# A three-layer max-aggregation graph network: edge arrays moved to POOL's queue, the lane table to PSUM, 49 node tiles, a shorter carry

## The chip, the cores and the metric

The kernel runs on one core of one Trainium2 chip. The metric is device time in microseconds (us). The core has five engines with queues of their own: PE (TensorE, matmuls), DVE (VectorE), ACT (ScalarE), POOL (GpSimd) and SP (SyncE, which only issues DMAs here), and 16 DMA engines that all queues share. Engines meet through semaphores. SBUF and PSUM are the on-chip memories, both with 128 partitions.

## What is computed

There are 6250 nodes with 128 features and 200000 edges `(src, dst)` sorted by `dst`. Cut to what matters:

```python
def conv(x, src, dst, Wl, bl, Wr):
    agg = segment_max(x[src], dst, num_segments=6250)   # max over a node's incoming edges
    agg = where(isfinite(agg), agg, 0.0)                # nodes without edges
    return agg @ Wl + bl + x @ Wr

h = maximum(layernorm(x), 0.0)
h = leaky_relu(conv(h, src, dst, Wl1, bl1, Wr1), 0.01)  # 128 -> 256
h = leaky_relu(conv(h, src, dst, Wl2, bl2, Wr2), 0.01)  # 256 -> 256
h = leaky_relu(conv(h, src, dst, Wl3, bl3, Wr3), 0.01)  # 256 -> 128
return x + h
```

## The kernel before, in words

**Tiling.** The edge list is cut into 512 runs of 391 edges: four chains (`CHAINS`) of 128 partitions. One column of work is one edge from each of 128 runs, so a layer has 4 x 391 = 1564 columns. A column is fetched by one indirect DMA on POOL's queue (L343): 128 indices from `stage` choose 128 rows of the feature table in HBM, and they land in `ring`, which holds 56 columns in 7 blocks of 8. A step is one turn of the ring; a layer has 28 steps, the last with 52 columns. Over three layers that is 4692 gathers.

**The scan.** For each group of four columns DVE adds a restart row (0 or the lowest float, from `restart_ps` in PSUM) to the previous group, L617, writing PSUM, and takes the maximum with the new group, L638. SP writes each finished group to a log in HBM (L1014, L1018). DVE also copies the indices of later blocks into `stage` (L606).

**The picks.** In the first 25 steps of layer 0, DVE also builds, once a step, the matrices by which PE finds each node's run: `pick_from` (L586) compares the lane table `lane` (0 to 255, in SBUF) with `pick_bounds` (SBUF) and writes into `own`; `pick_not_below` (L593) does the same with the upper bounds; `pick_below` (L601) subtracts one from the other, in bf16. Each goes over 128 x 1024 elements.

**A layer's end.** When the log is complete, POOL gathers four `patch` tiles (L360). Beside it runs the carry from run to run: PE turns the last group (L845), DVE scans it (L703, `carry_scan`), DVE adds the row `join_row[:, 0]` to the scan shifted by one (L709, `incoming`), and PE turns it back (L851). DVE takes the maximum with `patch` (L713), SP stores it (L1025). Then POOL gathers the last log row of each node, one DMA for each tile of 128 nodes (L370), 50 tiles. Tiles go in pairs: PE turns (L864), DVE masks and guards (L721, L731), PE multiplies by `Wl` (L876), DVE adds the node's own part and takes the leaky ReLU (L738, L749, in the last layer L753 and L762), SP stores (L1031). POOL's next layer waits for all these stores.

**The start.** SP issues the five loads of `x` (L984, 640 KB each), with `dst` after the first (L986) and `src` after the last (L987), then eight loads of one word per run (L992, `prev_last` and `next_first`), nine loads of weights, two small stores, and the five stores of the normalised features (L1004), each when its ten tiles are done. DVE computes the statistics (L411, L414), ACT normalises 8 tiles of ten (L907) and DVE the other two (L428, L431). DVE then takes the differences that tell whether `dst` is sorted (L443, L445, L448), PE sums them over partitions (L786), and all engines that may have to sort read the answer. DVE lays out `src` (L511), fills `stage` (L513) and prepares bounds, restart rows and join rows (L519 to L567) while POOL may begin gathering. POOL's first gather waits for the five stores and for `stage`. The rows of `x` are padded to 6400, 50 tiles; `out` has as many rows.

POOL waits at the head of each block of eight gathers, which is this piece:

```python
pool.wait_ge(block_scanned, ...)
if not first:
    pool.wait_ge(logged[b], ...)
pool.sem_inc(gathers_open, 1)
```

## Time and profile before

| | us |
|---|---|
| median of 3 runs | 6219.27 (6217.3 to 6219.34) |
| the profiled execution | 6222.6 |
| its span, first to last instruction | 6220.9 |
| busy, POOL / DVE / PE / ACT | 4632.6 / 2902.1 / 706.5 / 232.1 |
| share of the 16 DMA engines, gathers' queue / SP's and ACT's | 31.0% / 23.2% |
| indirect DMAs issued by POOL: gathers L343 / patch L360 / ends L370 | 4692 / 12 / 150 |

The median comes from executions without a profile, the rows further down from the one profiled execution. "Busy" counts an instruction from its start to its end; for a DMA on POOL's queue this is the time in which POOL writes it out, not the time in which the bytes move. A row of the timeline gives the start, the duration, engine, line, operation, output and input, and in brackets how long the engine stood idle before it and what ended that. "issue" means that the profile shows nothing that the engine waited for.

### The profile page before, as it was taken

Reading aid. Unit: us, or ns where it says so; the run is one execution under the profiler, and the core shown is the slowest. Engines: PE = TensorE matmul, PEld = TensorE weight load, DVE = VectorE, ACT = ScalarE, POOL = GpSimd, SP = SyncE. Lnnn points to the kernel's source line nnn. Section 1 sums busy time; section 2 is a strip of 40 time slices with the busy share of each in tenths; the row PEclk is TensorE's granted clock in tenths of the full one; section 3 lists DMA queues with packets and bytes.
Section 4 is the critical chain, followed back from the end, with each engine's and each line's share of the span. In section 5 each row is a group of like instructions: output and inputs, shape, how many; then the busy total and the mean of one; then the engine's idle time right before and its main releaser. Section 6 shows DMA issues by size and latency. Waiting matters only on the chain. (4 is left out here: it accounts for less than half of the span.)

```text
span 6220.9 us, 24572 instructions
## 1 busy us (share of the span) xinstructions
PE 706.5 (11%) x2258; PEld 407.3 (7%) x2258; DVE 2902.1 (47%) x3636; ACT 232.1 (4%) x675; POOL 4632.6 (74%) x4861
## 2 busy tenths in 40 slices
PE   0110011111000680000000000047000000000003
PEld 0000000000000340000000000035000000000002
DVE  5333333333333555555555555565555555555556
ACT  1000000000000110000000000012000000000001
POOL 5777777777777677777777777767777777777776
PEclk8555555555555655555555555565555555555556
DMA  4333333333333576666666666667666666666665
GB/s 131 104 106 106 104 103 105 106 105 104 106 104 103 153 240 210 210 209 212 209 211 209 210 209 209 211 195 252 209 211 209 209 210 209 209 210 211 209 211 166
DMA packets 436613, 1089.93 MB, mean 175 GB/s; under 512 B 101509, under 2 KB 155018, under 8 KB 436586
## 3 DMA queue, kind: packets, MB, share of 16 engines
q0 software_dynamic: 207104, 530.50, 31.0%
q1 hardware_dynamic: 206266, 539.48, 23.2%
q10 hardware_dynamic: 23216, 19.67, 1.0%
q14 instruction: 20, 0.16, 0.0%
q8 instruction: 7, 0.11, 0.0%
HBM read 555.78 MB, written 533.46 MB: 175 GB/s over the span
## 5 line engine op out<-in xcount | busy, mean ns | idle before, releaser
L343 POOL DMA_INDIRECT ring<-features,stage x4692 | 4475.1, 954 | 1491.1 <-issue 1384.2
L638 DVE TENSOR_TENSOR ring<-banks,ring 128x1024 f32<-128x1024 f32 (+1 forms) x1173 | 1226.2, 1045 | 3093.4 <-DMA ring<-features,stage 3076.0
L617 DVE TENSOR_TENSOR banks<-ring,banks 128x1024 f32<-128x1024 f32 (+1 forms) x1173 | 1232.4, 1051 | 37.6
L845 PE MATMUL banks<-ident,ring 128*128 128x128 f32 x20 | 5.0, 428 | 3755.5 <-DVEq L650 3755.5
L827 PE MATMUL banks<-dst_low,own 128*128 128x394 bf16 x200 | 99.2, 496 | 1492.7 <-DVE own L601 1492.7
L845 PEld LDWEIGHTS banks<-ident,ring 128*128 128x128 f32 x20 | 3.9, 222 | 3756.9 <-DVEq L650 3533.0
L811 PE MATMUL banks<-wr,h_turned 128*128 128x256 f32 (+1 forms) x500 | 207.3, 557 | 97.7 <-ACT h_turned L932 97.7
L975 ACT ACTIVATE agg<-zeros 128x512 f32<-128x512 f32 x75 | 47.3, 630 | 3962.2 <-PE banks L876 3962.2
L370 POOL DMA_INDIRECT ring<-running_max_log,end_row x150 | 145.2, 968 | 63.4 <-issue 44.8
L606 DVE COPY stage<-edges 128x8 int32 (+1 forms) x588 | 137.5, 234 | 84.9 <-DVE banks L617 25.8
L813 PE MATMUL banks<-b,ones 1*128 1x256 f32 (+1 forms) x300 | 143.7, 575 | 0.0
L811 PEld LDWEIGHTS banks<-wr,h_turned 128*128 128x128 f32 x500 | 122.7, 302 | 160.8 <-ACT h_turned L932 151.8
L827 PEld LDWEIGHTS banks<-dst_low,own 128*128 x200 | 27.6, 138 | 1536.1 <-issue 1534.4
L876 PE MATMUL banks<-wl,agg 128*128 128x256 f32 (+1 forms) x500 | 113.4, 370 | 2.0 <-DVE agg L731 1.9
L828 PE MATMUL banks<-dst_high,own 128*128 128x394 bf16 x200 | 97.9, 489 | 0.0
L803 PE MATMUL banks<-ident,h_in 128*128 128x128 f32 x250 | 85.4, 425 | 27.6 <-DMA h_in<-features 27.6
L948 ACT ACTIVATE signs<-banks,node 128x391 bf16<-128x391 f32 x50 | 29.4, 588 | 1571.4 <-PE banks L828 1571.3
L876 PEld LDWEIGHTS banks<-wl,agg 128*128 128x128 f32 x500 | 87.1, 213 | 12.0 <-DVE agg L731 5.0
L813 PEld LDWEIGHTS banks<-b,ones 1*128 1x128 f32 x300 | 67.4, 278 | 65.1 <-issue 65.1
L864 PE MATMUL banks<-ident,ring 128*128 128x128 f32 x250 | 60.4, 322 | 75.5 <-DMA ring<-running_max_log,end_row 73.3
L721 DVE TENSOR_SCALAR finite<-banks 128x512 int32<-128x512 int32 (+1 forms) x75 | 44.9, 598 | 47.1 <-PE banks L864 46.5
L941 ACT ACTIVATE own<-banks 128x256 f32 (+2 forms) x150 | 52.2, 348 | 367.4 <-PE banks L813 367.4
(104 smaller groups left out, 563.7 us busy)
## 6 DMA issues: line engine op xcount, KB each, us to landing
running_max_log<-ring SPq DMA_DIRECT2D x782, 512.0 KB, 3.3
running_max_log<-ring SPq DMA_DIRECT2D x391, 256.0 KB, 2.2
ring<-features,stage POOLq DMA_INDIRECT x4692, 2.8
features<-h_out SPq DMA_DIRECT2D x50, 256.0 KB, 2.3
h_in<-features ACTq DMA_DIRECT2D x100, 128.0 KB
ring<-x SPq DMA_DIRECT2D x5, 640.0 KB, 8.8
features<-ring SPq DMA_DIRECT2D x5, 640.0 KB, 7.2
h_in<-features ACTq DMA_DIRECT2D x50, 64.0 KB
```

Of the source, the lines that this page charges most:

```text
L343: pool.indirect_dma_start(ring[:, c * w:(c + 1) * w], None, tables[l], bass.IndirectOffsetOnAxis(ap=stage[:, b, u:u + 1].bitcast(U32), axi ...
L370: pool.indirect_dma_start(ring[:, t * w:(t + 1) * w], None, logs[w], bass.IndirectOffsetOnAxis(ap=end_row[:, t:t + 1].bitcast(U32), axis=0 ...
L606: dve.tensor_copy(stage[:, b, :], src_t[:, bass.ds((i + ahead) * RING_COLS + b * BLOCK_COLS, BLOCK_COLS)]).then_inc(block_scanned, 1)
L617: dve.tensor_tensor(sum_ps[:, 0:CHAINS * w].rearrange("p (h f) -> p h f", h=CHAINS), group(g - 1).rearrange("p (h f) -> p h f", h=CHAINS), ...
L638: dve.tensor_tensor(group(g), sum_ps[:, 0:CHAINS * w], group(g), ALU.max).then_inc(turn, 1)
L803: turn = pe.transpose(turn_ps[0][:, c * P:(c + 1) * P], h_in[p][:, c * P:(c + 1) * P], ident[:, :])
L811: pe.matmul(mm_ps[p][:, 0:n], h_turned[p][:, c, :], wr_sb[l][:, c, :], start=(c == 0), stop=False)
L813: pe.matmul(mm_ps[p][:, 0:n], ones[0:1, :], b_sb[l][:, :], start=False, stop=True).then_inc(own_mm, 1)
L827: pe.matmul(sel_ps[p][:, 0:RUN + 3], chosen, dst_low[:, h, :], start=(h == 0), stop=False)
L828: mm = pe.matmul(sel_ps[p][:, 0:RUN + 3], chosen, dst_high[:, h, :], start=False, stop=(h == CHAINS - 1))
L864: turn = pe.transpose(turn_ps[b][:, t * w + c * P:t * w + (c + 1) * P], ring[:, k * w + c * P:k * w + (c + 1) * P], ident[:, :])
L876: mm = pe.matmul(mm_ps[b][:, t * n:(t + 1) * n], agg[b][:, t * w + c * P:t * w + (c + 1) * P], wl_sb[l][:, c, :], start=(c == 0), stop=(c ...
```

## The change

- `x` is alone at the head of SP's queue, followed by the weights. `dst`, the neighbour words and `src` are issued by POOL. The eight neighbour loads become four: two of 127 partitions with four words each, two of three words.
- POOL takes the differences of neighbouring `dst` (int32 subtract, 128 x 1560 and 128 x 4). DVE takes their minimum and compares it with 0.
- ACT normalises 7 tiles of ten. The other three are POOL's now: three `tensor_scalar` and one maximum over 384 columns for each of the five shares. A first `Sqrt` of ACT stands before the wait for constants.
- `lane_ps`, a copy of the lane table, lies in PSUM bank 5 beside `restart_ps`; L586 and L593 read it in place of `lane`.
- `END_TILES` is 49: 49 gathers of ends in each layer, the last pair has one tile, and `own`, `h_in`, the intermediate tables and `out` follow.
- The carry: `joins` goes into `dst_high` (an offset of `NO_NODE` where a run doesn't join), so the row `join_row[:, 0]`, L709 and half of L562 to L567 go. `carry_scan` is one column longer, and PE turns it back directly.
- POOL opens each layer with one list of waits and then the gathers, without `sem_inc`; the first step of each layer is outside the loop; the waits for `h_stored` and `logged` are in reversed order; the `sem_inc` before L370 goes.

```diff
-ACT_TILES = 8
+ACT_TILES = 7
+    END_TILES = -(-nodes // P)
+    PAIR_TILES = [min(2, END_TILES - 2 * q) for q in range(PAIRS)]
...
+        lane_ps = banks[:, 5, BANK - 2 * P:BANK]
...
+            pool.dma_start(dst_runs, dst.rearrange("(h p) j -> p h j", p=P)).then_inc(order_loaded, DMA)
+            pool.wait_ge(const_done, 2)
+            with nc.allow_non_contiguous_dma(reason="one word of each run of edges"):
+                for dest, there in run_neighbours(dst):
+                    pool.dma_start(dest, there).then_inc(order_loaded, DMA)
+            pool.dma_start(src_runs.rearrange("p (h j) -> p h j", h=CHAINS),
+                           src.rearrange("(h p) j -> p h j", p=P)).then_inc(src_loaded, DMA)
+
+            pool.wait_ge(order_loaded, (LOADS - 1) * DMA)
+            pool.tensor_tensor(rises_runs[:, :, 1:RUN], dst_runs[:, :, 1:RUN], dst_runs[:, :, 0:RUN - 1],
+                               ALU.subtract).then_inc(order_checked, 1)
+            pool.tensor_tensor(rises_runs[:, :, 0], dst_runs[:, :, 0], prev_last[:, :],
+                               ALU.subtract).then_inc(order_checked, 1)
+
+            for s in range(TAIL_STEPS):
+                share = slice(s * TAIL_TILES + ACT_TILES, (s + 1) * TAIL_TILES)
+                pool.wait_ge(norm_ready, 2 * (s + 1))
+                for k in range(share.start, share.stop):
+                    pool.tensor_scalar(h0_all[:, k, :], x_all[:, k, :], rstd[:, k:k + 1], shift[:, k:k + 1],
+                                       ALU.mult, ALU.add).then_inc(h0_scaled, 1)
+                pool.wait_ge(h0_scaled, (TAIL_TILES - ACT_TILES) * (s + 1))
+                pool.tensor_scalar(h0_all[:, share, :], h0_all[:, share, :], 0.0, None,
+                                   ALU.max).then_inc(h0_rest_done, 1)
...
+                        for b in reversed(range(STORES)):
+                            pool.wait_ge(h_stored[b], PER_OUT * l)
+                        pool.wait_ge(block_scanned, SIGNED * l + 1)
+                        pool.wait_ge(logged[0], LOGGED[0] * l)
...
-                pool.sem_inc(ends_open, 1)
-                for t in range(TILES):
+                for t in range(END_TILES):
...
-                    dve.tensor_tensor(pick_slot(i), lane[:, :].unsqueeze(1).to_broadcast(across),
+                    dve.tensor_tensor(pick_slot(i), lane_ps.unsqueeze(1).to_broadcast(across),
...
                 for c in range(kc):
-                    dve.tensor_tensor_scan(carry_scan[:, c, :], join_row[:, 1, :],
+                    dve.tensor_tensor_scan(carry_scan[:, c, 1:RUNS + 1], pass_row[:, :],
                                            carry_ps[:, c * RUNS:(c + 1) * RUNS], 0.0,
-                                           ALU.add, ALU.max).then_inc(join_step, 1)
-                for c in range(kc):
-                    before = sum(s[0] for s in shapes[:l]) // P
-                    dve.wait_ge(join_step, before + c + 1)
-                    dve.tensor_tensor(incoming[:, c, 1:RUNS], carry_scan[:, c, 0:RUNS - 1],
-                                      join_row[:, 0, 1:RUNS], ALU.add).then_inc(incoming_ready, 1)
+                                           ALU.add, ALU.max).then_inc(carried_on, 1)
```

## Rows read from the trace of the kernel before

**Rows 1.** The page, groups by line: count, busy and mean ns, idle before by releaser
```profile
L343 POOL DMA_INDIRECT ring<-features,stage x4692 | 4475.1, 954 | 1491.1 <-issue 1384.2
```
**Rows 2.** Groups of POOL from 60 to 1805 us, then from 2130 to 4080 us
```profile
L343 POOL DMA_INDIRECT ring<-features,stage x1369 | 1329.5, 971 | 417.2 <-issue 376.1 <-DVE stage L606 41.1
...
L343 POOL DMA_INDIRECT ring<-features,stage x1560 | 1474.8, 945 | 475.2 <-issue 475.2
```
**Rows 3.** Timeline in step 24 of layer 0: start, us, engine, line, operation
```profile
1781.34 1.22 DVE L586 TENSOR_TENSOR own<-lane,pick_bounds 128x1024 f32 x1
1781.62 1.75 POOL L343 DMA_INDIRECT ring<-features,stage  x1 [0.30 <-issue]
...
1802.89 0.68 DVE L601 TENSOR_TENSOR own<-own,not_below 128x1024 bf16 x1
1803.15 1.24 POOL L343 DMA_INDIRECT ring<-features,stage  x1 [0.30 <-issue]
```
**Rows 4.** Timeline in layer 2: a gather beside the scan's maximum
```profile
6126.94 1.22 DVE L638 TENSOR_TENSOR ring<-banks,ring 128x1024 f32<-128x1024 f32 x1 [4.92 <-DMA ring<-features,stage]
6127.75 0.95 POOL L343 DMA_INDIRECT ring<-features,stage  x1 [0.30 <-issue]
```
**Rows 5.** Timeline in step 1 of layer 0: the one pick without a longer gather
```profile
139.33 1.26 DVE L586 TENSOR_TENSOR own<-lane,pick_bounds 128x1024 f32 x1
139.34 0.94 POOL L343 DMA_INDIRECT ring<-features,stage  x1 [0.31 <-issue]
```
**Rows 6.** Timeline of SP's queue at the start
```profile
13.39 4.54 SPq L992 DMA_DIRECT2D next_first<-dst  x1
...
25.51 8.21 SPq L1004 DMA_DIRECT2D features<-ring  x5
```
**Rows 7.** Stretches of the start: last three columns PEclk, DMA share, GB/s
```profile
2.00:18.00 16.00, 0.00 (x0) 0.00 (x0) 12.79 (x89) 6.24 (x15) 0.00 (x0) 1.00 1.09 303
18.00:22.00 4.00, 0.00 (x0) 0.00 (x0) 3.86 (x26) 3.47 (x11) 0.00 (x0) 1.00 0.17 11
22.00:26.00 4.00, 0.00 (x0) 0.00 (x0) 3.86 (x26) 3.47 (x11) 0.00 (x0) 1.00 0.82 235
26.00:38.00 12.00, 0.59 (x2) 0.50 (x2) 8.83 (x19) 5.44 (x15) 0.00 (x0) 1.00 0.98 280
```
**Rows 8.** Timeline of the start: ACT's last tiles, the order check, stage, the first gather
```profile
25.18 6.26 ACT L907 ACTIVATE ring<-ring,shift,rstd 128x128 f32<-128x128 f32 x16
...
27.32 1.78 DVE L443 TENSOR_TENSOR edges<-own 128x1560 f32<-128x1560 int32 x1
...
35.69 0.19 DVE L513 COPY stage<-edges 128x48 int32<-128x48 int32 x1
...
40.13 1.36 POOL L343 DMA_INDIRECT ring<-features,stage  x1 [38.65 <-DMA features<-ring]
```
**Rows 9.** Timeline: DVE's preparation beside the fourth gather
```profile
44.22 2.91 DVE L551 TENSOR_TENSOR edges<-own 128x1560 f32<-128x1560 int32 x1
44.41 4.53 POOL L343 DMA_INDIRECT ring<-features,stage  x1 [0.30 <-issue]
```
**Rows 10.** Timeline: POOL's widest elementwise instruction of before
```profile
0.98 0.34 POOL L261 IOTA lane_i<- 128x256 int32 x1 [0.40 <-POOLq L1067]
```
**Rows 11.** Timeline of layer 0's end: last two tiles on PE, last projection
```profile
2114.96 0.30 PE L864 MATMUL banks<-ident,ring 128*128 128x128 f32 x1 [0.90 <-DMA ring<-running_max_log,end_row]
...
2116.47 0.33 PE L864 MATMUL banks<-ident,ring 128*128 128x128 f32 x1 [1.21 <-DMA ring<-running_max_log,end_row]
...
2118.27 2.07 PE L876 MATMUL banks<-wl,agg 128*128 128x256 f32 x4 [0.59 <-DVE agg L731]
```
**Rows 12.** Groups with shapes apart: an end operation of DVE over two tiles and over half the width
```profile
L738 DVE TENSOR_TENSOR z_sum<-banks,own 128x512 f32<-128x512 f32 x50 | 34.0, 680 | 6.2 <-PE banks L876 6.1
...
L738 DVE TENSOR_TENSOR z_sum<-banks,own 128x256 f32<-128x256 f32 x25 | 10.2, 407 | 0.4 <-PE banks L876 0.3
```
**Rows 13.** Timeline of layer 2's end: the patch's maximum
```profile
6143.84 1.22 DVE L713 TENSOR_TENSOR patch<-patch,banks 128x1024 f32<-128x1024 f32 x1 [4.63 <-DMA patch<-running_max_log,patch_row]
```

More of the change, by code:

```diff
@@ L33, with gnn_program @@
 TILE_MASK = 0x7FFFFF80
-def gnn_program(nc, x, src, dst, weights, out):
+def gnn_program(nc, x, src, dst, weights, out, nodes):
     NODES, F_IN = x.shape
@@ L347, in gather @@
                             ).then_inc(landed[b], DMA)
-                if l == 0:
-                    gather(0, True, False)
-                with pool.Fori(1 if l == 0 else 0, STEPS - 1) as i:
+                gather(0, True, False)
+                with pool.Fori(1, STEPS - 1) as i:
                     gather(i, False, False)
                 gather(STEPS - 1, False, True)
-                for b in range(BLOCKS):
+                for b in reversed(range(BLOCKS)):
                     pool.wait_ge(logged[b], LOGGED[b] * (l + 1))
@@ L961, in keep_pair @@
                             count_run(j, p)
-                    for p in range(2):
-                        keep_turned(j, p, more)
+                    for p in range(PAIR_TILES[j] if isinstance(j, int) else 2):
+                        keep_turned(j, p, p < loads)
                         keep_own(j, p)
@@ L984, in _ @@
                 sp.dma_start(x_all[:, t, :], x_rows[:, t, :]).then_inc(x_loaded[s], DMA)
-                if s == 0:
-                    sp.dma_start(dst_runs, dst.rearrange("(h p) j -> p h j", p=P)).then_inc(edges_loaded, DMA)
-            sp.dma_start(src_runs.rearrange("p (h j) -> p h j", h=CHAINS),
-                         src.rearrange("(h p) j -> p h j", p=P)).then_inc(edges_loaded, DMA)
-            sp.wait_ge(const_done, 2)
-            with nc.allow_non_contiguous_dma(reason="one word of each run of edges"):
-                for dest, there in run_neighbours(dst):
-                    sp.dma_start(dest, there).then_inc(edges_loaded, DMA)
             for l, (wl, bl, wr) in enumerate(weights):
@@ L1071 @@
     }
-    out = nc.dram_tensor("out", (rows, arrays["L0_gnn_Wl3"].shape[1]), F32, kind="ExternalOutput").ap()
+    out = nc.dram_tensor("out", (-(-nodes // P) * P, arrays["L0_gnn_Wl3"].shape[1]), F32, kind="ExternalOutput").ap()
     weights = [tuple(given[name] for name in layers[3 * l:3 * l + 3]) for l in range(3)]
-    gnn_program(nc, given["x"], given["src"], given["dst"], weights, out)
+    gnn_program(nc, given["x"], given["src"], given["dst"], weights, out, nodes)
     r = run_bass_kernel_spmd(nc, [arrays], core_ids=[0])
```

213 lines of the change are left out of this document (113 added, 100 removed).

## The prediction

> **What bounds the kernel now.** I read the page's busy shares first, then the groups by line, the chain of waits, and POOL's timeline in full. The reader is to see in [rows 1] that the 4692 gathers hold POOL almost end to end: 4475.1 us busy plus 1384.2 us of "issue", the 0.30 us that stand between two gathers whatever DVE does. A gather and its gap take 0.945 + 0.30 = 1.25 us [rows 2], and 4692 + 12 + 150 indirect DMAs at 1.25 us are 6065 us of a span of 6220.9. The change touches none of this except three gathers. What it can move is the other 156 us: the start up to the first gather, 40.1 us [rows 8]; gathers made longer by DVE; and three layer ends, in which POOL waits for logs, patch and stores. DVE, PE and ACT have slack everywhere else, so time saved on them counts only in the start and at the three ends.
>
> **1. The lane table in PSUM.** In the stretch with picks the mean gather takes 971 ns, in layer 1 945 ns [rows 2]; over 1369 gathers that is 1369 x 0.026 = 36 us. The rows of [rows 3] show where they lie: a gather that begins while L586 runs takes 1.75 in place of 0.945 us and ends 0.81 us after L586 has ended. The same happens with L593. I went through all of POOL's timeline: of the 50 instructions of L586 and L593, 49 have such a gather, and their excess sums to 33.7 us (0.69 each). The 25 of L601 add 4.0 us (0.16 each). A gather that begins beside L638 keeps its 0.95 us [rows 4]; so do all 785 that begin during L638 and all 1043 during L617, to within 0.003 us in the mean. L586, L593 and L601 read two operands in SBUF; L638 and L617 read one in SBUF and one in PSUM, over as many elements in as much time (1.22 us). With `lane_ps` L586 and L593 get the form of L638. So this term is **-33.7 us**; L601 keeps its 4.0. Bounds: 0 if the stall has another cause, -37.7 if L601's gather falls clear as well. I take -33.7 because the 785 gathers are of exactly the new form.
>
> The Trainium skill (SBUF — State Buffer, "Who interferes with whom") speaks for and against. It says that a DVE instruction with two SBUF inputs contends with a GpSimd instruction that reads SBUF; but also that `tensor_tensor` was not seen stalling a DMA, inferred from descriptor generation needing the write side. By the second the stalls would have another cause and the term would be 0. The rows of [rows 5] fit the first: where the gather began with L586 rather than inside it, it kept its 0.94 us and L586 took 1.26, as if the gather only reads something, its indices, at its very beginning.
>
> **2. The start.** Both [rows 6] and [rows 7] show SP's queue as the limit: eight loads of single words keep SP until 20.7 us (one is held for 4.54 us), the DMA engines stand at a share of 0.17 from 18 to 22 us, and the first feature store is issued only at 25.51, though ACT had finished its first eight tiles long before. From 26 to 38 the stores run at a share of 0.98: bandwidth. The last tile is ready at 25.18 + 6.26 = 31.44 us [rows 8], the first gather starts at 40.13. After: the same bytes must move, 16 us for `x`, `dst` and `src`, 3.3 us for weights (4 us at 0.82), 12 us for stores [rows 7], so 2 + 16 + 3.3 + 12 = 33.3 us, and what lies between the end of that traffic and the first gather before (38.2 to 40.1, 1.9 us) stays: 35.2 us, **-4.9 us**. This holds the last tile even if it is as late as before. What is late next: `stage`, at 35.88 before [rows 8]. Its chain on DVE loses L443 (1.78 us) and L428 and L431, 0.9 us in each of five shares, so about 29.6 us: covered. If it stayed, the gain would be 3.4.
>
> The added work on POOL: six DMAs (1024 rows of 1564 bytes, 1022 single words), a wait for five of them, 1564 differences, then 3 x 128 and 384 elements in each of five shares. No row shows a plain DMA or an arithmetic instruction on POOL. An issue costs at least a gather's 1.25 us; 512 descriptors could cost four times 128, 4.7. So POOL has issued them at 1.5 + 6 x 1.25 = 9 us, or at 1.5 + 4 x 4.7 + 2 x 1.25 = 23 us. IOTA wrote 256 elements in 0.34 us [rows 10], 1.3 ns each; the differences at that rate are 2.1 us, at twice it 4.2; a share of the tiles (768 elements) 1.0 to 2.0 us plus four instructions' overhead, say 1.4 to 2.8. Early end: POOL is through the differences at 12 and follows the statistics. Late end: 27 us, then five shares of 2.8, 41 us, and the last store (2.4 us of traffic, 1.9 of the rest) opens the gathers at 45.3, +5.2 us. I take the early side, as a gather writes 128 random rows and a plain copy is no harder; the cover is then the store traffic. Queued behind POOL's waits are the sort question and the first gather; behind them the whole kernel. Range of the term: -6.5 to +5.2.
>
> The Trainium skill (GPSIMD Engine Reference, "Performance versus the Vector engine") gives 4497 ns for a two-input operation of 2048 fp32 elements; by it the differences would be an estimated 3.4 us, inside these bounds, and the sum would be unchanged, as they are covered.
>
> Preparation on DVE (L519 to L567) overlaps the first gathers as before: a gather held for 4.53 us [rows 9] is 3.6 us of loss that I leave, since `stage` and the first gather move together. It is 0 if DVE is through first.
>
> **3. 49 tiles.** Each layer's last pair becomes one tile. At layer 0's end the last tile reaches PE at 2116.47, the one before it at 2114.96 [rows 11]: 1.5 us. Then half of the last projection (2.07 / 2 = 1.0 us), and twice 680 - 407 = 0.27 us on DVE [rows 12]: -3.05 us. Layer 1 has the same shapes after the turn and wider ones before: -3.1. In layer 2 the output is half as wide: 1.25 for the gather, 0.6 for the projection, 4 x 0.14 on DVE: -2.4. Sum **-8.6 us**, between -5 (only the gathers and a half of the rest) and -11.
>
> **4. The carry.** L713 waits for the patch DMA, not for the carry [rows 13]: the turned carry has been ready for over two microseconds, so the shorter chain is worth nothing. The L709 instructions, with two SBUF operands, lengthen three patch gathers by 0.33 us in all: **-0.3 us**.
>
> **5. POOL's waits.** Dropped `sem_inc` at six places and reversed waits at five: each some 0.04 us either way, and the unrolled first steps have the form that layer 0 already has. 0, between -1.5 and +1.5.
>
> **Sum.** -4.9 - 33.7 - 8.6 - 0.3 = -47.5 us. Against the profiled execution's own 6222.6: 6175.1. That execution lies 3.3 us above the median of 6219.27, so the median should be 6172.
>
> **Rivals.** (A) The forecast, 6172. (B) POOL is late at the start: 23 us of issuing, slow shares, first gather at 45.3: the sum is -37.4, 6182. For it: no row prices plain DMAs there. Against: it needs both upper bounds. (C) The lane table doesn't free the gathers, so the change doesn't do what it is built for: -13.8, 6205.5. Against it stand 1828 undisturbed gathers. (D) Slower: POOL writes single words one at a time, at a price p for 128. The start carries 2046 rows and words, 16 times 128; the kernel is slower than before once 16p exceeds the 47.5 us saved plus the 8 x 0.945 us or so that fits under the store traffic, from p = 3.4 us, over three times a gather's 0.945. At p = 5 us the time would be 6219 - 47.5 + 72 = 6244. Against: a gather also has 128 separate rows.
>
> **How the numbers follow.** Chances: A 0.80, B 0.07, C 0.08, D 0.03, anything else 0.02. The range takes A with its bounds (the start from -6.5 to +5, the ends from -11 to -5, L601's 4 us) and B, and leaves out C and D: 6160 to 6188. A measurement of this kernel can tell about 0.2%, 12 us, from no change. A and B are faster by more; C lies at the bound and goes half to each. Faster 0.92, same 0.05, slower 0.03.
>
> **What would show it.** The mean gather from 60 to 1805 us falls to 0.948 us, with only L601's 25 gathers longer; L586 and L593 keep 1.22 us. The first gather starts near 35 us, the first feature store before 18, and the DMA share has no hole from 18 to 22. POOL's differences end before 16 us. L713 still waits for the patch. The idle time before each next layer's first gather falls by about 1.5 us. The prediction is wrong if gathers still stretch beside L586, or if POOL's own shares are the last thing before the stores.

## The result, and the profile after

The changed kernel takes 6191.97 us (median of 6 runs, 6189.52 to 6194.53) against 6218.44 us (6 runs, 6217.3 to 6219.34) for the kernel before: 26.5 us less, a ratio of 0.9957 with a 95% interval of 0.9946 to 0.9969. The sign was forecast; the size was not: 6172 us was forecast, in a range that ends at 6188. Its profiled execution took 6190.32 us, its span 6188.5 us. Some of the runs below (e5 to e10, e5r, e8r, g1, g2) were made while every kernel, the one before too, took some 800 us longer, and the profiled executions of e2, e3, f1, f2 and f3 are 10 to 17 us longer than the others of their kernels, so times are medians set against the kernel before as it ran beside them, and from traces only starts, gaps and single rows are read.

The page's first view (busy us and count by engine) and the gathers' group (count, busy and mean ns, idle time before them):

```profile
PE 696.7 (11%) x2214; PEld 398.1 (6%) x2214; DVE 2891.8 (47%) x3613; ACT 228.5 (4%) x665; POOL 4623.9 (75%) x4886
...
L383 POOL DMA_INDIRECT ring<-features,stage x4692 | 4435.1, 945 | 1450.4 <-issue 1400.8
```

The mean gather fell from 954 ns [rows 1] to 945 ns, 40 us over 4692 gathers. So the lane table did what it was to do (3.6 us of the 40 are another stall, told below). The timeline of POOL's start shows what took the gain back (start, us, engine, line, operation, and in brackets the idle time before it and what ended it):

```profile
1.62 0.96 POOL L273 DMA_DIRECT2D own<-dst  x1
2.60 5.17 POOL L277 DMA_DIRECT2D prev_last<-dst  x2
21.83 5.10 POOL L277 DMA_DIRECT2D next_first<-dst  x2 [14.06 <-issue]
26.92 0.79 POOL L278 DMA_DIRECT2D own<-src  x1
35.26 2.78 POOL L282 TENSOR_TENSOR edges<-own 128x1560 int32<-128x1560 int32 x1 [7.55 <-DMA next_first<-dst]
...
38.18 1.31 POOL L291 TENSOR_SCALAR ring<-ring,rstd,shift 128x128 f32<-128x128 f32 x3
...
52.97 3.92 POOL L291 TENSOR_SCALAR ring<-ring,rstd,shift 128x128 f32<-128x128 f32 x3
56.98 2.44 POOL L294 TENSOR_SCALAR ring<-ring 128x384 f32<-128x384 f32 x1
63.41 1.10 POOL L383 DMA_INDIRECT ring<-features,stage  x1 [3.99 <-DMA features<-ring]
```

The first gather starts at 63.41 us; before it started at 40.13 [rows 8]. The `x3` of a row groups three instructions. Three things are to be seen. POOL gets from its second load of single words to its third only after 14.06 us in which it does nothing that the profile names. The last words land at 35.26 us, 8.3 us after their issue ended. And POOL's five shares of the normalisation stand behind the differences in its queue: they run from 38.18 to 59.42 us, long after ACT had finished its own last tile (31.83 us), and only then can the last store go.

The two loads in each of those `x2` rows differ: 508 words (2.0 KB) take 4.62 us to issue, three words 0.57. The first pair lands 18.0 and 14.3 us after the start of its issues (view of the DMAs: KB, us to landing), the later one at 21.5 us, and POOL's next load begins at 21.83:

```profile
prev_last<-dst POOLq DMA_DIRECT2D x1, 2.0 KB, 18.0
prev_last<-dst POOLq DMA_DIRECT2D x1, 0.0 KB, 14.3
```

So the hold ends just after the first two word loads have landed (in e4, below, at 21.6 and 21.96 us). No wait of the program stands there; why POOL is held is not shown.

DVE's timeline says why the shares are slow and why one stall is gone:

```profile
38.23 1.78 DVE L471 TENSOR_REDUCE least_rise<-edges 128x1 f32<-128x1564 int32 x1 [11.43 <-POOL edges L284]
...
53.78 2.91 DVE L579 TENSOR_TENSOR edges<-own 128x1560 f32<-128x1560 int32 x1
```

DVE, too, waits for POOL's differences (11.43 us), and then does its preparation beside POOL's shares. L579 is L551 of [rows 9]; it now ends before the first gather, so no gather is held by it.

From the first gather to the end of the last indirect DMA, the kernel before took 6170.75 us (40.13 to 6210.88) and the changed one 6116.20 us (63.41 to 6179.61): 54.6 us less. The start costs 23.3 us more, what follows the last indirect DMA 1.1 us less. That is the whole result in three numbers: -54.6 + 23.3 - 1.1 = -32.4 us of span, between two profiled executions that stand 4.2 us above and 1.7 us below their medians.

In step 24 a pick's last part now looks like this (before: [rows 3]):

```profile
1786.74 0.68 DVE L627 TENSOR_TENSOR own<-own,not_below 128x1024 bf16 x1
1787.21 1.03 POOL L383 DMA_INDIRECT ring<-features,stage  x1 [0.30 <-issue]
```

and the two parts that read the lane table from PSUM keep their length (L612 and L619 are L586 and L593):

```profile
L612 DVE TENSOR_TENSOR own<-banks,pick_bounds 128x1024 f32 x25 | 30.3, 1213 | 0.0
L619 DVE TENSOR_TENSOR not_below<-banks,pick_bounds 128x1024 bf16<-128x1024 f32 x25 | 30.3, 1213 | 0.0
```

Between 60 and 1800 us no gather of the changed kernel takes over 1.3 us; before, 49 did.

### The profile page after: what moved, and what is told of

Same layout as the page of the kernel before. It is cut to its first block and busy times, and to the rows that moved or that the text cites. A ratio compares the mean times of both kernels' runs of the same rounds, so it can differ in the third digit from the quotient of the medians.

```text
span 6188.5 us, 24424 instructions
## 1 busy us (share of the span) xinstructions
PE 696.7 (11%) x2214; PEld 398.1 (6%) x2214; DVE 2891.8 (47%) x3613; ACT 228.5 (4%) x665; POOL 4623.9 (75%) x4886
## 5 line engine op out<-in xcount | busy, mean ns | idle before, releaser
L851 PEld LDWEIGHTS banks<-dst_low,own 128*128 (+1 forms) x200 | 27.8, 139 | 1511.4 <-issue 1449.1
L827 PE MATMUL banks<-ident,h_in 128*128 128x128 f32 x245 | 83.4, 423 | 26.5 <-DMA h_in<-features 26.5
L977 ACT ACTIVATE own<-banks 128x256 f32 (+3 forms) x147 | 51.2, 349 | 360.4 <-PE banks L837 360.4
L743 DVE TENSOR_SCALAR finite<-banks 128x512 int32<-128x512 int32 (+2 forms) x75 | 44.4, 591 | 40.5 <-PE banks L897 39.9
## 6 DMA issues: line engine op xcount, KB each, us to landing
ring<-x SPq DMA_DIRECT2D x5, 640.0 KB, 10.4
```

Source lines behind the costliest of these rows:

```text
L827: turn = pe.transpose(turn_ps[0][:, c * P:(c + 1) * P], h_in[p][:, c * P:(c + 1) * P], ident[:, :])
L851: pe.matmul(sel_ps[p][:, 0:RUN + 3], chosen, dst_low[:, h, :], start=(h == 0), stop=False)
```

## The experiments

The theory after this reading was: all the parts do about what the prediction said, except for the start, and there it is the single words on POOL's queue that come late. Its rivals: POOL's arithmetic is too slow for the start; or the later parts (49 tiles, waits) lost time that the lane table gained.

**The two ends of the account.** `e1_start_before` is the changed kernel with the whole start of before (loads on SP, eight word loads, differences on DVE, 8 tiles on ACT and 2 on DVE). `e2_lane_only` is the kernel before with the lane table in PSUM and nothing else:

```diff
+        lane_ps = banks[:, 5, BANK - 2 * P:BANK]
...
+            dve.tensor_copy(lane_ps, lane_i[:, :]).then_inc(const_done, 1)
...
-    dve.tensor_tensor(pick_slot(i), lane[:, :].unsqueeze(1).to_broadcast(across),
+    dve.tensor_tensor(pick_slot(i), lane_ps.unsqueeze(1).to_broadcast(across),
```

> The changed kernel with the start of before: dst, src and eight loads of single words on SP's queue, differences on DVE, the tiles shared by ACT (8 of ten) and DVE (2). Everything behind the start stays changed. Theory (the start alone cost what was missing; the first gather moved from 40.13 to 63.41 us): the first gather is back at about 40 us, the 3.6 us stall of the fourth gather comes back, and the time is 6192 - 23.3 + 4 = 6173 us. Rival (the traces of one execution each mislead, the rest of the kernel saved less than its 54.6 us): above 6180.

> The kernel before with the lane table in PSUM and nothing else. Theory (a gather that begins inside a DVE instruction with two SBUF operands waits for it): the 49 long gathers beside L586 and L593 are gone, 6218.4 - 33.7 = 6184.7 us, with L601's 25 left. Rival (the gain between first and last gather came from the other parts): 6218.

Measured: `e1_start_before` 6172.45 us (6171.41 to 6174.09), 0.9926 [0.9909, 0.9942] of before; `e2_lane_only` 6186.38 us, 0.9948 [0.9931, 0.9964]. Before took 6218.29 beside them. So the lane table alone is worth 31.9 us, and no gather of e2 between 60 and 1800 us takes over 1.3 us. And the start of the change costs 19.5 us against the old start (6191.97 - 6172.45). The prediction had it gain 4.9. In `e1_start_before` the first gather and its stall are back where they were:

```profile
39.43 1.42 POOL L362 DMA_INDIRECT ring<-features,stage  x1 [37.95 <-DMA features<-ring]
...
44.90 4.30 POOL L362 DMA_INDIRECT ring<-features,stage  x1 [0.30 <-issue]
```

**The two suspects of the start, one at a time.** `e3_words_sp` moves only the four word loads to SP's queue, behind `x`; `e4_shares_dve` leaves the words on POOL and gives POOL's shares back to ACT (8 tiles) and DVE (2 tiles):

```diff
-                    pool.dma_start(dest, there).then_inc(order_loaded, DMA)
+                    sp.dma_start(dest, there).then_inc(words_loaded, DMA)
```

```diff
-ACT_TILES = 7
+ACT_TILES = 8
...
-                    pool.tensor_scalar(h0_all[:, k, :], x_all[:, k, :], rstd[:, k:k + 1], shift[:, k:k + 1],
+                    dve.tensor_scalar(h0_all[:, k, :], x_all[:, k, :], rstd[:, k:k + 1], shift[:, k:k + 1],
```

> The changed kernel with only the four loads of single words issued by SP, behind x; dst and src stay on POOL's queue, and so do the differences and the three tiles of ten. Theory 1 (single words written by POOL itself are what held the start: two issues of 2.6 us, 14.1 us without an instruction, the last word at 35.3 us): the words land before 24 us, the differences end by 27, five shares of some 3 us follow, the first gather starts near 45 and the time is 6192 - 18 = 6174. Theory 2 (four words for each partition are slow on any queue): the words land at 33 or later and the time stays within 3 us of 6192.

> The changed kernel with the tiles shared by ACT (8 of ten) and DVE (2) again; words and differences stay POOL's. Theory 1 (the words come first, at 35.3 us, and POOL's 21.2 us of tiles after them are the second part): the stores are through by 36 us, the first gather waits for stage alone, which was at 44.6, and starts near 45.5: 6192 - 18 = 6174 us; the stall beside DVE's preparation comes back, some 4 us: 6178. Rival (the tiles hide behind the words and the order check): no change, 6192.

Measured: 6181.26 and 6181.32 us, both 0.994 [0.9923, 0.9956]. Each takes back 10.7 us, about half of the loss, and both less than was expected. The first rows of `e3_words_sp`, and then of `e4_shares_dve`, say where each stays short:

```profile
24.93 2.79 POOL L280 TENSOR_TENSOR edges<-own 128x1560 int32<-128x1560 int32 x1 [21.58 <-DMA next_first<-dst]
...
53.12 1.07 POOL L381 DMA_INDIRECT ring<-features,stage  x1 [3.99 <-DMA features<-ring]
```

```profile
38.72 2.78 POOL L282 TENSOR_TENSOR edges<-own 128x1560 int32<-128x1560 int32 x1 [10.90 <-DMA next_first<-dst]
...
48.82 1.33 POOL L374 DMA_INDIRECT ring<-features,stage  x1 [7.16 <-DVE stage L538]
```

With the words on SP the differences still start only at 24.93 us: neither of the two forecasts for e3 (before 24, or 33 and later) came. Part of that is SP's place, for SP reaches the words only at 12.86 us. Its queue (timeline) shows the rest:

```profile
12.86 7.21 SPq L1023 DMA_DIRECT2D prev_last<-dst  x2
20.11 3.59 SPq L1023 DMA_DIRECT2D next_first<-dst  x2
```

These four loads end at 23.70 us; before's eight, from the same place (12.94 us), end at 20.63. So on SP's queue the new shape costs some 3 us, and most of the loss on POOL's queue is that queue's own. With the shares on DVE (e4) the gathers wait for `stage`, the end of DVE's chain behind the late differences. The two losses are one chain: late words, then the work queued behind them.

**The shape of the word loads.** The change and e3 take nearly all words in two loads over 127 partitions with four words in each partition (the neighbour of partition p is in p - 1 or p + 1, so one end is missing); before had eight loads of one word per partition, six of them over 128. `e9_words_wide` loads the same words, still on POOL's queue, in six loads over 128, 112, 15 and again 15, 112, 128 partitions:

```diff
-            pairs = [(prev_last[1:P, :], own_runs[0:P - 1, :, RUN - 1]),
-                     (prev_last[0:1, 1:CHAINS], own_runs[P - 1:P, 0:CHAINS - 1, RUN - 1]),
+            flat = runs.rearrange("r j -> (r j)")
+            part_h = P * RUN
+            last = flat[part_h - 1:part_h - 1 + (CHAINS - 1) * part_h].rearrange("(h p j) -> p h j", p=P, j=RUN)
+            pairs = [(prev_last[:, 1:CHAINS], last[:, :, 0]),
+                     (prev_last[16:P, 0:1], own_runs[15:P - 1, 0:1, RUN - 1]),
+                     (prev_last[1:16, 0:1], own_runs[0:15, 0:1, RUN - 1]),
...
```

> After with one thing changed: the single-word loads on POOL's queue (prev_last and next_first) are cut so that a load spans 128, 112 or 15 partitions and none spans 127 (six loads for four); the words loaded are the same. Theory (a 127-partition load of single words is spread over few DMA engines, and that holds the queue): the words are on the chip before 20 us and not at 35, POOL's shares stay where they contend with the statistics, the first gather starts between 47 and 55 us for after's 63.4, and the time is 6175 to 6183 us. Rival (single words in POOL's queue are slow whatever the shape, since POOL writes them one by one): next_first still lands at 33 to 37 us, the first gather stays within 3 us of 63.4, and the time is 6189 to 6195 us.

In its trace the differences start at 11.78 us in place of 35.26, and the first gather at 33.97 in place of 63.41. Both are earlier than was expected: with the words early POOL's shares are no longer slow either. Its time was 6994.84 beside 7017.39 us, 0.9966 [0.9954, 0.9977]. It was run again, as `f1_words_wide`, beside 6218.84 us for the kernel before:

> The kernel after with the single-word loads cut so that none spans 127 partitions, again, beside runs of before at its usual time. Theory (the shape of these loads is the whole of the missed term): the first gather starts at 34 us for after's 63.4, and with 1 us of time for each us of the start, less 3.4 us for the stall of a gather beside VectorE's preparation that comes back, the time is 6192.0 - 29.4 + 3.4 = 6166 us (6163 to 6170). Rival (the shape is only a part of it, or the statistics of x and the shares collide once they run side by side in a shorter start): 6172 to 6182 us.

Measured: 6169.02 us, 0.9919 [0.9903, 0.9936]. POOL's start in `f1_words_wide`:

```profile
1.61 0.96 POOL L279 DMA_DIRECT2D own<-dst  x1
2.58 1.92 POOL L283 DMA_DIRECT2D prev_last<-dst  x3
4.50 1.92 POOL L283 DMA_DIRECT2D next_first<-dst  x3
6.41 0.80 POOL L284 DMA_DIRECT2D own<-src  x1
12.05 2.78 POOL L288 TENSOR_TENSOR edges<-own 128x1560 int32<-128x1560 int32 x1 [4.84 <-DMA next_first<-dst]
14.79 0.20 POOL L290 TENSOR_TENSOR edges<-own,prev_last 128x4 int32<-128x4 int32 x1
14.97 1.32 POOL L297 TENSOR_SCALAR ring<-ring,rstd,shift 128x128 f32<-128x128 f32 x3
...
29.50 1.17 POOL L300 TENSOR_SCALAR ring<-ring 128x384 f32<-128x384 f32 x1
35.13 2.04 POOL L389 DMA_INDIRECT ring<-features,stage  x1 [4.47 <-DMA features<-ring]
...
41.27 4.27 POOL L389 DMA_INDIRECT ring<-features,stage  x1 [0.31 <-issue]
```

This is the start that the prediction had drawn: all DMAs (here eight) issued by 7.2 us, the differences through at 15, the shares following the statistics, the first gather at 35.1 (forecast 35.2). Six word loads in the new shape take 3.84 us to issue, where four in the old one took 24.3 us (2.60 to 26.92). The time fell by 23.0 us. The 28.3 us between the first gathers split in two: the differences start 23.2 us earlier, and the five shares take 15.7 us (14.97 to 30.67, with 2.8 us of waits for the statistics) where they took 21.2 beside DVE's preparation. Some 3.3 us go back to the stall beside L551's successor, which returned (4.27 us).

What in the cut does it? It changes several things at once: no load spans 127 partitions, and none has over 384 words or three a partition (508 and four in the change). `g1_words_127x1` keeps the 127 partitions and loads one word per partition, four loads and a remainder for each array; `g2_words_eight` puts before's eight loads on POOL's queue:

```diff
-            pairs = [(prev_last[1:P, :], own_runs[0:P - 1, :, RUN - 1]),
...
+            for h in range(CHAINS):
+                pairs.append((prev_last[1:P, h:h + 1], own_runs[0:P - 1, h:h + 1, RUN - 1]))
+                pairs.append((next_first[0:P - 1, h:h + 1], own_runs[1:P, h:h + 1, 0]))
...
```

> The kernel after with each of its two large word loads (127 partitions, four words each) cut into four over the same 127 partitions with one word each, all still on POOL's queue. Theory (it is the 127 partitions): the same 1016 words are as late as in after, POOL is held again for 10 us or more among the loads, the differences start at 30 us or later, the first gather at 58 us or later, and the time is 6187 to 6194 us. Rival (it is the number of words in one load, 508 there and 384 at most in the quick cut): the differences start before 16 us, the first gather at 34 to 38 us, and the time is 6167 to 6173 us.

> The kernel after with the eight word loads of before on POOL's queue: one word per partition, six loads over 128 partitions and two over 127. Theory (only a load over 127 partitions is slow, each by about a quarter of what one with four words costs): the differences start between 14 and 22 us, later than the 12 us of the wide cut but far earlier than the 35 of after, the first gather at 36 to 46 us, and the time is 6170 to 6180 us. Rival (it is the number of words in one load): the same as the wide cut, differences at 12 to 13 us, first gather at 34 to 36 us, 6167 to 6171 us.

POOL's timeline of `g1_words_127x1` (one of its eight loads over 127 partitions, then the last small one, and what follows):

```profile
2.60 0.59 POOL L279 DMA_DIRECT2D prev_last<-dst  x1
...
7.30 0.52 POOL L279 DMA_DIRECT2D next_first<-dst  x1
7.81 0.78 POOL L280 DMA_DIRECT2D own<-src  x1
13.23 2.78 POOL L284 TENSOR_TENSOR edges<-own 128x1560 int32<-128x1560 int32 x1 [4.64 <-DMA next_first<-dst]
...
33.91 1.95 POOL L385 DMA_INDIRECT ring<-features,stage  x1 [4.57 <-DMA features<-ring]
```

My theory fell: on POOL's queue a load over 127 partitions with one word in each is as quick as any other. In g2 the differences start at 12.26 and the first gather at 35.22 us. The ratios of the two are 0.9965 [0.9951, 0.9979] and 0.9962 [0.9948, 0.9977], like that of e9, 0.9966. What is shown is this: 1016 of the words in two loads of 127 x 4 are late and hold POOL's queue; the same words in eight loads of 127 x 1, in eight of 127 or 128 x 1, or in six of up to 128 x 3, are not. Whether the number of words in one load decides, or 127 partitions together with several words, was not tried on POOL's queue.

The records of single DMA packets in the same traces say more. On POOL's queue, f1's words show as 32 packets of 96 bytes and 32 of 28, the bytes of the words themselves, moved between 8.8 and 10.4 us. g1's eight show as 128 packets of 32 bytes, 4096 in all for 4064 of words. The change's two large loads show as 224 packets of 256 bytes and 32 of 240: 65024 bytes, sixteen times the 4064 that they load. They are under way from 11.4 to 19.6 and from 27.1 to 34.6 us, up to 16 at a time, and one takes 0.43 us in the mean where one of f1's takes 0.02. On SP's queue it is another matter: each word is a packet of 4 bytes there, and e3's two loads never have more than four packets under way at once, mostly two, at 170 words per us. Before's loads over 127 partitions with one word each go like this too; its six over 128 have up to 12 under way, and f2's of 128 x 3 (below) up to 22. So on SP's queue the 127 partitions do decide, for one word as for four, and on POOL's it is the sixteenfold traffic that belongs to 127 x 4. Why POOL's queue makes it is open.

**Is a microsecond of the start a microsecond of time?** The first gather's start, plus what the gathers up to 60 us take over 0.945 us each ("stretched"), gives an effective start; the median minus it should be the same in all kernels with 49 tiles and the new waits:

| kernel | first gather | stretched | effective start | median | difference |
|---|---|---|---|---|---|
| after | 63.4 | 0.2 | 63.6 | 6192.0 | 6128.4 |
| e3 words on SP | 53.1 | 0.2 | 53.3 | 6181.3 | 6128.0 |
| e4 shares on DVE | 48.8 | 4.2 | 53.0 | 6181.3 | 6128.3 |
| e1 start of before | 39.4 | 3.8 | 43.3 | 6172.5 | 6129.2 |
| f1 wide words | 35.1 | 4.5 | 39.6 | 6169.0 | 6129.4 |
| f2 (below) | 33.2 | 3.7 | 36.9 | 6166.4 | 6129.5 |

The last column holds within 1.5 us over 27 us of start. So the start is on the critical path for all of its length, and nothing further along gives the gain back.

**POOL's waits.** Back to the other parts: in the traces the gaps at the layers' ends had shrunk by more than the tiles explain. `e5_waits_old` and `f3_waits_old` are one kernel: the start of before, and POOL's old waits (order, form and increments); `e8_sem_inc` and `f4_sem_inc` are another, where only the increment between the waits and the first gather is put back, at each opening and each end (the second diff, which the first pair has too):

```diff
-                        if first and b == 0:
-                            open_layer()
-                        else:
...
-                for b in reversed(range(BLOCKS)):
+                for b in range(BLOCKS):
```

```diff
+                    pool.sem_inc(gathers_open, 1)
```

> e1_start_before with POOL's waits as before: the semaphore increments between the waits and the first gather of a layer and before the ends, the waits in rising order, the first step of layers 1 and 2 inside the loop. Theory (an instruction between the wait and the DMA keeps POOL from preparing the DMA while it waits: after a wait at a layer's opening POOL started 1.04 us after the stores had landed before, 0.3 us after the change): some 0.7 us at each of three openings and 0.5 to 0.7 us at three ends and three patches, 4 to 5 us in all: 6172.5 + 4.5 = 6177. Rival (the prediction's: 0.04 us each, the idle time shrank by the tiles alone): within 1 us of 6172.5.

> e1_start_before with only the semaphore increments put back, at the opening of each layer and ahead of the ends; the order of the waits and the unrolled steps stay as changed. Theory (the increment is what costs): the idle time ahead of those six places rises by 0.6 to 0.8 us each, 6172.5 + 4 = 6176.5, nearly e5_waits_old. Rival (the order of the waits costs): no change, 6172.5.

> After with the whole start of before (6172.45 us in its own run) and with all of POOL's old waits. Theory (each layer opening, each patch and each end has 0.6 to 0.8 us more between the last landing and the indirect DMA that it lets go; seven to eight such places): 6177 us (6175 to 6179). Rival (the shorter gaps come from the 49 tiles alone): 6171 to 6174 us.

> After with the whole start of before, and of POOL's old waits only the increment between the wait and the indirect DMA, at the openings of the layers and at their ends. Theory (the increment alone costs 0.55 us at each of these places, as the gap ahead of the ends' gathers, 18.4 to 18.6 us in three with it and 16.6 to 16.9 us in three without, has it): half of the whole, 6174.5 to 6176.5 us. Rival (the order and the number of waits carry it, not the increment): 6171 to 6174 us.

The first of each pair, and one more repetition of each (`e5r_waits_old`, `e8r_sem_inc`), gave 0.9981 [0.9971, 0.9991] and 0.9984 [0.9974, 0.9993] for all the old waits, 0.9979 [0.997, 0.9989] and 0.9977 [0.9965, 0.9988] for the increments: too near to each other to tell anything. The second of each pair: `f3_waits_old` 6179.61 us, 0.9936 [0.992, 0.9953]; `f4_sem_inc` 6175.56 us (6175.36 to 6175.91), 0.9931 [0.9914, 0.9947]; to be set against 6172.45 (6171.41 to 6174.09) of `e1_start_before`. Each set against the kernel before beside it: -39.2, -43.3 and -45.8 us. The medians stand in the order that was expected, but the intervals of all three ratios overlap, so the gaps in the traces have to carry the reading. The views of POOL's waits (total us, times, longest), of f4, then of `e1_start_before`, then of f3, show the places:

```profile
POOL ring L389 <- DMA running_max_log<-patch: 18.5, 3, 6.6
POOL patch L379 <- DMA running_max_log<-ring: 18.1, 3, 6.6
```

```profile
POOL patch L378 <- DMA running_max_log<-ring: 18.1, 3, 6.6
POOL ring L387 <- DMA running_max_log<-patch: 16.9, 3, 6.1
```

```profile
POOL patch L370 <- DMA running_max_log<-ring: 20.1, 3, 7.3
POOL ring L380 <- DMA running_max_log<-patch: 18.5, 3, 6.6
```

The increment costs 0.5 us at each of the three ends (18.5 against 16.9) and 0.9 us at the first opening (first gather 40.32 against 39.43 us): 2.5 us in all, as much as the medians differ. At the openings of layers 1 and 2 it shows nothing: gaps of 8.4 and 10.3 us with it, 9.8 and 10.4 without. The old order adds 0.65 us at each patch (20.1 against 18.1). That leaves some 2 us of f3's 6.6 that no gap shows; this rest is open, and so is why the order matters.

**A version below both.** `e6_best_pool` put `dst` (after the third part of `x`), the words and `src` back on SP, VectorE on the differences, POOL on the shares, and the stores ahead of the weights; `e7_best_dve` was the same with ACT 8 and DVE 2 tiles. `e10_best_wide` and `f2_best_wide` are e6 with the wide word loads:

```diff
+                if s == 2:
+                    sp.dma_start(dst_runs, dst.rearrange("(h p) j -> p h j", p=P)).then_inc(order_loaded, DMA)
...
+                for dest, there in run_neighbours(dst):
+                    sp.dma_start(dest, there).then_inc(order_loaded, DMA)
...
-            pool.wait_ge(order_loaded, (LOADS - 1) * DMA)
-            pool.tensor_tensor(rises_runs[:, :, 1:RUN], dst_runs[:, :, 1:RUN], dst_runs[:, :, 0:RUN - 1],
...
+            dve.wait_ge(order_loaded, (LOADS - 1) * DMA)
+            dve.tensor_tensor(rises_runs[:, :, 1:RUN], dst_runs[:, :, 1:RUN], dst_runs[:, :, 0:RUN - 1],
```

> The changed kernel with another start: SP issues x with dst after its third load, the four loads of single words and src, then the five feature stores as they come ready, and the weights only behind them; DVE takes the differences; POOL has only its three tiles of ten. Theory (the start is bound by SP's queue and then by the DMA engines; 4 us of weights leave the path, POOL's tiles run beside the statistics at 2.5 us a share): stage is ready near 31 us and the first gather starts near 33 in place of 39.4: 6172.5 - 6 = 6166 us. Rival (POOL's tiles are slow beside DVE's instructions, up to 6.4 us a share as in the changed kernel, and are the last before the stores): first gather at 38 or later, 6171 to 6174.

> As e6_best_pool, with the tiles shared by ACT (8 of ten) and DVE (2). Theory: DVE has 4.5 us more work before the differences, stage is ready near 35 us and the first gather starts near 36.5: 6169 us, 3 us behind e6_best_pool. Rival of e6: this one is ahead of it by some 2 us or more, as nothing waits for POOL.

> The candidate: edge arrays and the words in the wide cut on SyncE's queue, VectorE takes the differences, POOL the shares, the stores of the table ahead of the weights. In its profile the first gather stood at 32.8 us. Theory (the start is worth its microseconds): 1.2 us earlier than the kernel with the wide words on POOL's queue, so 6165 us (6162 to 6169), below both kernels and below after with the start of before (6172.5). Rival (what is gained at the start waits at the end of the first layer): 6170 to 6175 us.

In the traces of e6 and e7 the first gather started at 36.91 and 37.11 us, for e6 later than the 33 that was expected; their ratios were 0.9965 [0.9954, 0.9976] and 0.9971 [0.9961, 0.998], which overlap, so that e6 is ahead of e7 by 3 us is not shown. That of e10 was 0.9956 [0.9942, 0.9971]. `f2_best_wide` measured 6166.37 us, 0.9915 [0.9899, 0.9932]: 52.5 us below the kernel before and 25.6 below the changed one. SP's queue (timeline) still shows the first group of words:

```profile
9.51 5.39 SPq L1025 DMA_DIRECT2D prev_last<-dst  x3
14.94 1.24 SPq L1025 DMA_DIRECT2D next_first<-dst  x3
16.23 0.49 SPq L1026 DMA_DIRECT2D own<-src  x1
16.83 12.08 SPq L1032 DMA_DIRECT2D features<-ring  x5
```

The stores now begin at 16.8 us, not 25.5 [rows 6]. Its executions without a profile (6165.02 to 6166.43) lie below those of f1 (6167.58 to 6169.48), by about the 2.7 us by which the effective start is earlier.

## Why the prediction was wrong

Set against the kernel before beside it, each kernel gives one step of the account. The intervals of e2, e1, f3 and f4 overlap in part; steps of a few us are differences of medians:

| step | forecast | measured | from |
|---|---|---|---|
| lane table in PSUM | -33.7 | -31.9 | e2 |
| 49 tiles and the carry | -8.9 | -7.3 | e2 to f3 |
| POOL's waits | 0 | -6.6 | f3 to e1 |
| the start | -4.9 | +19.4 | e1 to after |
| sum | -47.5 | -26.5 (before rounding) | |

**What bounds the kernel: right.** The gathers follow each other without a hole, and only the start, the stretched gathers and the layer ends moved.

**Step 1, the lane table: right, in mechanism and size.** The picks' gathers fell clear once the two compares read one operand in SBUF and one in PSUM. The gathers beside L601 stayed a little long (1.03 us in the row above). The Trainium skill (SBUF — State Buffer, "Who interferes with whom") says, beside the rule that the prediction sets against it, that `tensor_tensor` was not seen stalling a DMA. The traces disagree with that sentence: with both operands in SBUF it stretched 49 gathers to 1.53 to 1.75 us [rows 3], and e2, in which nothing but that operand moved, has none of these.

**Step 2, the start: this step failed, by 24.3 us.** The failing sentences are the price of the word loads: "An issue costs at least a gather's 1.25 us; 512 descriptors could cost four times 128, 4.7", and "I take the early side, as a gather writes 128 random rows and a plain copy is no harder". The issue of 508 words took 4.62 and 4.57 us, close to the upper price, 4.7, that the prediction set aside. What the sum had no place for is what comes behind an issue: the 14.06 us in which POOL was held after the first two, and the 9 to 18 us until the words landed. The description of the change named the shape of the new loads ("two of 127 partitions with four words each"), and the prediction then priced them by their number of descriptors alone, although no row showed a load of that shape: the eight of before have one word per partition. f1, g1 and g2 issue as many words on the same queue without the hold.

[rows 6] was also read too simply. The 4.54 us were put down to the single words, as a cost that leaves SP when they leave. But in the changed kernel, where a weight load stands directly behind `x`, it is that one which is held (SP's queue, timeline; the last row is the feature stores, which had begun at 25.51 before and were forecast before 18):

```profile
0.88 10.90 SPq L1021 DMA_DIRECT2D ring<-x  x5
11.83 5.41 SPq L1023 DMA_DIRECT2D wr<-L_gnn_Wr  x1
...
40.85 19.02 SPq L1033 DMA_DIRECT2D features<-ring  x5
```

So the hold belongs to the place behind the loads of `x`, not to the words; what makes it is not shown. The traffic argument, 33.3 us plus 1.9, met the number as soon as the words were not late, 35.13 us in f1, but in part by luck. There ACT's last tile ends at 30.97 us and POOL's last share at 30.67, the last store goes behind them, and from 31 to 35.1 us the DMA engines stand at a share of 0.69, not 0.98. So the last tile and one store behind it set that start, and not the sum of the traffic alone.

The second half of the miss is the order in POOL's queue. The prediction named what was queued behind the wait, gave "POOL's own shares are the last thing before the stores" as a sign of being wrong, and put 1.4 to 2.8 us on a share; alone a share takes 2.5 us (1.31 + 1.17), inside this. Beside DVE's preparation, where the late words had pushed them, the five shares took 2.5 to 6.5 us each. This was in no term.

Of the rivals, B (POOL late, first gather at 45.3, 6182 us) had the mechanism, with too early a time: it was given 7%, and its bound was drawn from the issue only. D named the price of single words and its deciding point, 3.4 us for 128. By the rows it was 24.3 us for the eight 128s of words, 3.0 us each; D failed on the rows of `dst` and `src`, which cost it nothing like that (0.96 and 0.79 us for 512 rows each), and so the kernel was not slower. That the price hangs on the shape of the load, not on the number of words in all (0.48 us for 128 in f1), was in neither.

The Trainium skill has a rule that bears on this (DMA: Bandwidth & Descriptors, "Why a DMA increments its semaphore by 16 and not by 1"): a DMA is spread over the largest number of engines up to 16 that divides the slowest dimension of both its sides, so 16 for 128 or 112 partitions, 15 for 15, and one for 127. It makes an exception for some direct copies of POOL's queue, which it says use all engines at 127 too. The trace bears out the exception for one word per partition: in g1 eight such loads over 127 partitions are quick. On SP's queue the packets fit the rule: at most two to four under way for a load over 127 partitions, up to 12 for 128. For the two of 127 x 4 on POOL's queue one engine is not the cause, since up to 16 of their packets are under way at once; neither rule nor exception has the sixteenfold bytes. The same skill's figure for POOL's two-input operation (GPSIMD Engine Reference, "Performance versus the Vector engine"), from which the prediction had an estimate of 3.4 us for the differences, was a little high: the trace has 2.78 us, for int32.

The stall beside L551 was left at 3.6 us "since `stage` and the first gather move together", with "0 if DVE is through first". DVE was through first, because the shares held the gathers and not DVE; a gain of 3.6 us, inside the measured +19.4.

**Step 3, the tiles: right to 1.6 us (with step 4).** The last projection of layer 0 falls from 2.07 us [rows 11] to 0.70, and POOL's gaps before the next two layers from 11.2 and 12.6 us to 8.7 and 10.5 (f3).

**Step 4, the carry: right as far as the trace shows.** No run prices the 0.3 us. The patch's maximum still waits for the patch, in layer 2 for longer than before [rows 13]:

```profile
6114.32 1.22 DVE L734 TENSOR_TENSOR patch<-patch,banks 128x1024 f32<-128x1024 f32 x1 [5.12 <-DMA patch<-running_max_log,patch_row]
```

**Step 5, the waits: wrong by 6.6 us, the other way.** "Each some 0.04 us" was no reading of a row, but a count of instructions. The gaps at the ends had the answer: an increment between a wait and an indirect DMA costs 0.5 to 0.9 us. The two errors partly cancel; without this one the miss would have been larger.

**The range.** It ended at 6188 because the term of the start ended at +5.2, and that end was the worst case of a row of the wrong kind. A bound from an issue's duration doesn't bound the landing. One product of the working is off, 4854 x 1.25 us is 6067.5 and not 6065; nothing hangs on it.

## What to carry to other kernels

Before moving a DMA to another queue, read what it costs where it stands, from issue to landing, and carry that price along until a row shows that the queue and not the load makes it slow. Price a load by a row of the same shape: the same thousand words in two loads of 127 x 4 or in six smaller ones made 23 us of 6192. In an in-order queue, don't put a share of a pipeline (here the normalisation) behind a wait for something else; one late word delays it all. And where an indirect DMA is what everybody waits for, put nothing between its last wait and it.

## What the runs showed of the hardware

- Two loads of 127 partitions x 4 single words (and two of three words): on POOL's queue 5.17 and 5.10 us to write with 14.06 us of hold between, landing 9 to 18 us after issue, with sixteen times their bytes in the packet records; on SP's queue they take SP 10.8 us, the hold behind the loads of `x` included (e3). In loads of up to 128 x 3, 127 x 1 or 128 x 1: 0.52 to 0.64 us each on POOL, and 5.5 to 7.8 us to landing (f1, g1, g2).
- On SP's queue a load of single words over 127 partitions had two to four packets under way at once (170 words per us, e3), one over 128 up to 12 (before).
- The first DMA on SP's queue behind the five loads of `x` was held for 5.41 us (a weight load, in the changed kernel) or 4.33 us (the same, f1); before, it was the second load of words, 4.54 us.
- POOL's arithmetic: a subtraction of 128x1560 int32 2.78 us, a two-scalar operation over 128x128 about 0.44 us, a maximum over 128x384 1.17 us; beside DVE's preparation three of the second took up to 3.92 us in place of 1.31, and the third up to 2.44 (the changed kernel).
- A semaphore increment between the last wait and an indirect DMA on POOL: 0.5 us at the ends, 0.9 us at the first opening.
- A plain DMA of 512 rows of 1564 bytes costs POOL 0.79 to 0.96 us to issue, about as much as a gather of 128 rows (0.945).
